# A two-layer graph network: the place of the matrix-sum copy, its add, and the segment sums in the slot order of the edge stage

## The chip, the cores and the metric

The kernel runs on 1 core of one Trainium2 chip. The metric is the device time of one execution in microseconds. The kernel before took 1502.47 us (median of 3 runs, 1501.93 to 1503.01).

## What is computed

The reference has two layers over 1250 nodes with 512 features and 40000 edges, sorted by target node. Only the first is per edge and heavy:

```
h = relu(layernorm(x))
# layer 0
edge_feat = concat(h[src], h[dst], edge_attr)          # 40000 x 1088
m   = mish(mish(edge_feat @ W1 + b1) @ W2 + b2)        # 40000 x 512
agg = segment_sum(m, dst, 1250)
u   = mish(concat(h, agg) @ W3 + b3);  y = h + u @ W4 + b4
x   = x + layernorm(y) * gamma + beta
# layer 1
h   = relu(layernorm(x));  support = (h @ U * s) @ Vt
x   = x + relu(segment_sum(support[src] * w, dst, 1250) + bias)
```

All is float32 on input and output. The kernel multiplies in a rounded 32-bit format and keeps a high and a low part of each operand, so that one product takes three matmuls.

## The kernel before, in words

A prologue works out the node tables `A_tab` (h times the source part of W1) and `Bh_tab`, `Bl_tab` (the target part, high and low). Then comes the **edge stage** (`edge_narrow`, from line 839), which this change touches, then a node stage (W3, W4, norms), and the second layer's matrix product.

The edge stage takes the edges in **groups** of 512, each of 4 **units** of 128: 78 full groups and a tail of 64 edges. A unit number modulo 4 is called j here. Each engine runs its own list of **slots** (`slots`, `step` of each engine), one per unit, and in slot s it works on units at fixed distances from s:

- TensorE, slot s (`step`, L1203): `gathered(s+5)` transposes the gathered table rows into a `bp` bank (4 transposes, L1153), `products(s+5)` adds the two edge products there (L1161, L1165), `msg(s)` makes the second product of the message in bank `bm[j]` (12 matmuls, L1176), `adjacency(s)` adds the unit to the matrix sums in bank `pm` (L1186). After the slot in which a group has been complete for three slots, `seg` makes the group's segment sums in bank `bs` (four f32 products, L1199).
- ScalarE, slot s (`step`, L1285): the first activation of the first mish for unit s+5 (L1235, exp out of `bp`), the first of the second mish for unit s-1 (L1255, exp out of `bm`), then alternately L1259, L1238, L1261, L1241, L1263. Once a group: the cast L1277 (`cast`), the copy of half of the segment sums L1283 (`evac`), and the **copy of the matrix sums** L1270 (`adjacency`: from `pm`, the high parts, to `mev`).
- VectorE, slot s (`step`, L1411): `pre(s+4, 0)` ends the first mish (L1362, waits for ScalarE's L1241), `bias` refills a `bm` bank with b2 (L1381), `square` (L1352, between ScalarE's L1235 and L1238), `pre(s+4, 1)` (L1368), the one-hot columns for the matrix (L1387, L1388), `msg(s-2)` (L1375). Once a group: L1335, L1330, L1342, the add of the segment sums L1409 (`evac`), and the **add of the matrix sums** L1398 (`join`: `mev` += the low parts in `pm`, waits for the copy L1270).
- GpSimd, slot s: the low part `hTl` (L1078), the gathers (L1065), and the adds of `ev` and `mev` into the tables `agg_tab` (L1092) and `M_tab` (L1103) in HBM.

There is one bank `pm`: TensorE's first `adjacency` of a group (j = 0) waits until the join of the group before it is done (`wait(e, s_mev, u.group())`, L1184). There is one bank `bs`: `seg` waits for the add of the group before (`s_ev`, L1197). The order inside a slot is written out by hand in the `step` functions; the lags are the constants in lines 853 to 871. In slot terms, the copy L1270 of group g is issued in ScalarE's slot 4g+4, after L1235 of that slot, and the join in VectorE's slot 4g+4, after L1362 and L1381.

After the last unit, TensorE's slots MSGS and MSGS+1 (313 and 314) hold `xpart(e, 0, 0)` and `xpart(e, 0, 1)`, 12 matmuls each of the node stage (L336). The last full group's `seg` has its slot among them.

Of the kernel before, what the change touches and what calls it, by code (L numbers as in the profile page):

```python
# [34 lines left out]
SUB = 4  # L35
G = SUB * P
NG = -(-E // G)
FULL = E // G
# [800 lines left out]
def edge_narrow(work, scope, sem, k):  # L839
# [13 lines left out]
    PRE_AHEAD = 5  # L853
    ACT_MSG = 1
    DVE_PRE = 4
    DVE_MSG = 2
    SEG_LAG = 3
    CAST_AHEAD = 10
    PREP_AHEAD = {1: 10, 2: 9}
    NEAR_CAST = 8  # L860
# [6 lines left out]
    ACCS = 2  # L867
    MBUF = 2 * SUB
    ADJ_AHEAD = 1
    ADJ_EV_LAG = 4  # L870
    ADJ_LAG = {2: (6, 0), 0: (8, 1)}
    BACK = 2
    FIRST, LOOP0 = -10, 16
# [2 lines left out]
    PRES = 4 * NG  # L876
    MSGS = 4 * FULL + 1
# [3 lines left out]
    with st:  # L881
# [48 lines left out]
        def first(u):  # L930

            return u.reg is None and u.const < SUB
# [9 lines left out]
        def pick(u, start, steady):  # L942

            return start[u.const] if first(u) else steady[u.const % 2]
# [11 lines left out]
        def tail(u):  # L956

            return u.reg is None and u.const >= 4 * FULL
# [184 lines left out]
        @work.on("tensor")  # L1143
        def _(e):
            def gathered(u):
                j, p, w, bank = u.j, u.par, ETAIL if tail(u) else G, pick(u, start_bank, bp)
                if not first(u):
                    e.wait_ge(v_pre, free(u))
                if j == 0:
                    e.wait_ge(q_ga[p], u.pair(64, 16 if tail(u) else 64))  # L1150
                for t in range(SUB if w == G else 1):
                    r = min(P, w)
                    e.matmul(bank[:, t * P:t * P + r].bitcast(F32R), xg[p][0:r, t, j * P:(j + 1) * P], ident_r[0:r, 0:r],  # L1153
                             start=t == 0, stop=False, is_transpose=True, skip_group_check=True)

            def products(u):
                j, p, w, bank = u.j, u.par, ETAIL if tail(u) else G, pick(u, start_bank, bp)
                if j == 0:
                    e.wait_ge(q_win[p], u.pair(48, 48))
                    e.wait_ge(s_hot, u.group(1, 1))  # L1160
                e.matmul(bank[:, 0:w], eaW1[p][:, j * P:(j + 1) * P], M1[p][:, 0:w], start=False, stop=False,  # L1161
                         skip_group_check=True)
                if j == 0:
                    e.wait_ge(s_ealow, u.group(1, 1))
                e.matmul(bank[:, 0:w], eaW2[:, j * P:(j + 1) * P], M2[p][:, 0:w], start=False, stop=True,  # L1165
                         skip_group_check=True).then_inc(s_pre, 1)

            def msg(u):
                j, p, r = u.j, u.par, ETAIL if tail(u) else P
                e.wait_ge(v_bias, u.val(1, 1))  # L1170
                bank = bm[j]
                for c in range(KC):
                    if j == 0:
                        e.wait_ge(g_pre, u.val(1, c + 1))
                    for a, w in ((hTh, W2h), (hTl, W2h), (hTh, W2l)):
                        last = e.matmul(bank[0:r, :], a[p][:, c, j * P:j * P + r], w[:, c, :], start=False,  # L1176
                                        stop=c == KC - 1 and w is W2l, skip_group_check=True)
                last.then_inc(s_msg, 1)

            def adjacency(u):  # L1180

                i, r, o = u.const % 2, ETAIL if tail(u) else P, u.j // HSUB * 2 * EC
                if u.j == 0:
                    wait(e, s_mev, u.group())  # L1184
                e.wait_ge(v_adj, u.val(2, 2))
                e.matmul(pm[0:KEYS, o:o + 2 * EC], key[i][0:r, :], so[i][0:r, :, :].rearrange("p a n -> p (a n)"),  # L1186
                         start=u.j % HSUB == 0, stop=u.j % HSUB == HSUB - 1 or tail(u), skip_group_check=True)\
                 .then_inc(s_adj, 1)

            def seg(u):  # L1190

                p, last, r = u.par, tail(u), ETAIL if tail(u) else P
                n = 1 if last else SUB
                first = u + (1 - n)
                e.wait_ge(v_msg, u.val(1, 1))
                e.wait_ge(s_oh, u.group(1, 1))
                wait(e, s_ev, u.group())  # L1197
                for j in range(n):
                    m = e.matmul(bs[j * WIN:(j + 1) * WIN, :], oh[p][0:r, j, :], tm[(first.const + j) % MBUF][0:r, :],  # L1199
                                 start=True, stop=True)  # L1200
                m.then_inc(s_seg, 1)

            def step(s):  # L1203
                if (s + PRE_AHEAD).has(PRES):
                    gathered(s + PRE_AHEAD)
                    products(s + PRE_AHEAD)
                if s.has(MSGS):
                    msg(s)
                    adjacency(s)
                q = s + -SEG_LAG  # L1210
                if (q.j == SUB - 1 and q.has(4 * FULL)) or (q.reg is None and q.const == 4 * FULL):
                    seg(q)
                if s.reg is None and s.const in (MSGS, MSGS + 1):
                    xpart(e, 0, s.const - MSGS)

            e.wait_ge(c_tb, 3 * (NCH - 2) + 1)
            for j in range(SUB):
                gathered(At(None, j))
            for j in range(SUB):
                products(At(None, j))  # L1220
            slots(e, SUB - PRE_AHEAD, LOOP0, LOOP1, LAST, step)
            e.wait_ge(v_msg, MSGS)
            e.wait_ge(s_mev, NG)

        @work.on("scalar")
        def _(e):
# [58 lines left out]
            def step(s):  # L1285
                u, m, q, g = s + PRE_AHEAD, s + -ACT_MSG, s + -EV_LAG, s + -ADJ_EV_LAG
                c = s + CAST_AHEAD
                if near(s, NEAR_CAST):
                    c = s + NEAR_CAST
                for pre, k in ((1, 0), (0, 0), (0, 1), (1, 2), (0, 2), (1, 3), (0, 3)):  # L1290
                    if pre and u.has(PRES):
                        pre_chain(u, k)
                    if pre and k == 0 and g.j == 0 and g.has(MSGS):
                        adjacency(g)
                    if pre and k == 3 and c.j == 0 and c.has(4 * NG) and (c.reg is not None or c.const >= 4 * SUB
                                                                          or near(s, NEAR_CAST)):
                        cast(c)
                    if not pre and m.has(MSGS):
                        msg_chain(m, k)
                    if not pre and k == 0 and q.j == 0 and q.has(4 * FULL):  # L1300
                        evac(q)
# [19 lines left out]
        def _(e):  # L1321
# [72 lines left out]
            def join(u):  # L1394

                e.wait_ge(a_adj, u.group(1, 1))
                to, of = matrix(u, 1)
                e.tensor_tensor(to, of, to, ALU.add).then_inc(s_mev, 1)  # L1398
# [10 lines left out]
                e.tensor_tensor(ev[u.par][:], bs[n:2 * n, :], ev[u.par][:], ALU.add).then_inc(s_ev, 1)  # L1409

            def step(s):  # L1411
                u, m, v, f, a = s + DVE_PRE, s + -DVE_MSG, s + PRE_AHEAD, s + -(DVE_MSG + 1), s + -ADJ_EV_LAG
                if u.has(PRES):
                    pre(u, 0)
                if f.has(MSGS - SUB):
                    bias(f)
                if a.j == 0 and a.has(MSGS):
                    join(a)
                if v.has(PRES):
                    square(v)  # L1420
                if u.has(PRES):
                    pre(u, 1)
                for k in (1, 2):
                    g = s + PREP_AHEAD[k]
                    if near(s, NEAR_PREP[k]):
                        prep(s + NEAR_PREP[k], k)
                    elif g.j == 0 and g.has(4 * NG) and (g.reg is not None or g.const >= 4 * SUB):
                        prep(g, k)
                h = s + -ONE_LAG
                if h.j == 0 and h.has(MSGS) and not (h.reg is None and h.const <= SUB):  # L1430
                    onehot(h)
                if (s + ADJ_AHEAD).has(MSGS) and not (s.reg is None and s.const == 0):
                    adjacency(s + ADJ_AHEAD)
                if m.has(MSGS):
                    msg(m)
                q = s + -(EV_LAG + 2)
                if q.j == 0 and q.has(MSGS):
                    if tail(q):
                        e.wait_ge(s_seg, NG)
                        e.sem_inc(s_fin, 1)  # L1440
                    evac(q)
                if s.reg is None and s.const == MSGS - 3:
                    split_w3x(e)
# [25 lines left out]
            u = [At(None, j) for j in range(SUB + 1)]  # L1469
# [1059 lines left out]
```

## Time and profile before

| | |
|---|---|
| median of 3 runs | 1502.47 us |
| the profiled execution | 1502.91 us |
| its span in the trace | 1501.1 us |
| mean granted TensorE clock | 0.996 |
| PE busy | 1460.7 us (97%) |
| DVE busy | 1389.8 us (93%) |
| ACT busy | 1343.5 us (89%) |
| POOL busy | 1067.0 us (71%) |

PE is TensorE's matmuls, PEld its weight loads, DVE VectorE, ACT ScalarE, POOL GpSimd, SP SyncE. The busy shares overlap: the engines work side by side on different units. The profiled execution took 1.8 us more than its span, which is what lies around the program. The edge stage's loop fills the span from about 100 to 1375 us.

### The profile page before, as it was taken

What the parts mean: (1) busy time and instruction counts of PE and PEld (TensorE: products, weight loads), DVE (VectorE), ACT (ScalarE), POOL (GpSimd) and SP (SyncE); (2) the same over time, 40 slices, a digit from 0 to 9 for tenths busy, and PEclk for the clock granted to TensorE, in tenths of its full rate; (3) what the DMA queues carried; (4) which work ended last, traced back from release to release, by engine and by line L of the source; (5) the groups of instructions that cost most, each with busy time, mean ns of one, the idle gap of its engine ahead of it and who ended that gap; (6) DMA issues with size and microseconds to landing.
All of it is one profiled execution on the core that took longest, in us unless ns stands there. A gap on an engine that the chain in (4) does not pass through costs nothing.

```text
span 1501.1 us, 33053 instructions
## 1 busy us (share of the span) xinstructions
PE 1460.7 (97%) x7549; PEld 1124.8 (75%) x7549; DVE 1389.8 (93%) x2922; ACT 1343.5 (89%) x2587; POOL 1067.0 (71%) x978
## 2 busy tenths in 40 slices
PE   7989999999999999999999999999999999999998
PEld 6867777777777777777777777777777777777885
DVE  7879999999999999999999999999999999997776
ACT  5098999999999999999999999999999999997562
POOL 1267888788888878887887888778788888863220
PEclk9999999999999999999999999999999999999999
DMA  8867555454555545455545545554554555454764
GB/s 290 273 205 191 121 120 117 116 124 114 122 119 123 116 114 126 114 120 117 128 114 116 124 117 118 118 128 114 118 123 118 117 117 125 117 130 107 180 154 155
DMA packets 126036, 201.90 MB, mean 134 GB/s; under 512 B 32897, under 2 KB 58649, under 8 KB 126000
## 3 DMA queue, kind: packets, MB, share of 16 engines
q0 software_dynamic: 58528, 109.71, 33.8%
q1 hardware_dynamic: 67120, 91.24, 20.2%
q10 hardware_dynamic: 352, 0.52, 0.1%
q8 instruction: 16, 0.26, 0.1%
q14 instruction: 20, 0.16, 0.0%
HBM read 151.60 MB, written 39.54 MB: 127 GB/s over the span
## 4 chain that ended last, share of the span: by engine, by line
PE 76%; issue 8%; POOL 7%; ACT 3%; DVE 2%; POOLq 2%; DMA 1%; SPq 1%; DVEq 0%; ACTq 0%
PE bm L1176 43%; PE bp L1153 5%; PE bp L1161 5%; PE bs L1199 4%; PE bp L1165 4%; PE pm L1186 3%; PE pA L723 2%; PE po L2185 2%; PE pu L336 2%; PE pu L2163 2%; PE pB L723 2%; POOL hTl L1078 2%; POOL agg_tab L1092 2%; POOL xg L1065 2%; POOL M_tab L1103 2%
## 5 line engine op out<-in xcount | busy, mean ns | idle before, releaser
L1078 POOL TENSOR_TENSOR hTl<-tp,hTh 128x512 fp32r<-128x512 f32 (+1 forms) x314 | 410.7, 1308 | 196.5 <-DVE so L1388 193.8
L1176 PE MATMUL bm<-W2h,hTh 128*128 128x512 f32 x1252 | 494.4, 395 | 0.1
L1176 PE MATMUL bm<-W2h,hTl 128*128 128x512 f32 x1252 | 489.9, 391 | 0.0
L1176 PE MATMUL bm<-W2l,hTh 128*128 128x512 f32 x1252 | 489.5, 391 | 0.0
L1065 POOL DMA_INDIRECT xg<-A_tab,idx x305 | 320.7, 1051 | 71.0 <-issue 43.6
L1176 PEld LDWEIGHTS bm<-W2h,hTh 128*128 128x128 f32 x1252 | 235.4, 188 | 62.4 <-POOL hTl L1078 9.3
L1176 PEld LDWEIGHTS bm<-W2l,hTh 128*128 128x128 f32 x1252 | 235.6, 188 | 52.2
L1176 PEld LDWEIGHTS bm<-W2h,hTl 128*128 128x128 f32 x1252 | 235.8, 188 | 47.9
L1362 DVE SCALAR_TENSOR_TENSOR tp<-rp,bp 128x512 f32<-128x512 f32 (+1 forms) x314 | 213.0, 678 | 37.3 <-ACT rp L1241 28.8
L1352 DVE SCALAR_TENSOR_TENSOR rp<-rp 128x512 f32<-128x512 f32 (+1 forms) x314 | 214.9, 685 | 9.2 <-ACT rp L1235 2.7
L1238 ACT ACTIVATE rp<-rp 128x512 f32<-128x512 f32 (+1 forms) x314 | 195.3, 622 | 27.3 <-DVE rp L1352 23.3
L1375 DVE SCALAR_TENSOR_TENSOR tm<-rm,bm 128x512 f32<-128x512 f32 x313 | 211.6, 676 | 2.5 <-ACT rm L1263 2.5
L1381 DVE COPY bm<-b2b 128x512 f32<-128x512 f32 x309 | 211.6, 685 | 0.0
L1235 ACT ACTIVATE rp<-bp 128x512 f32<-128x512 f32 (+1 forms) x314 | 180.2, 574 | 30.5 <-PE bp L1165 30.5
L1259 ACT ACTIVATE rm<-rm 128x512 f32<-128x512 f32 x313 | 197.6, 631 | 7.5
L1263 ACT ACTIVATE rm<-rm 128x512 f32<-128x512 f32 x313 | 193.8, 619 | 0.1
L1261 ACT ACTIVATE rm<-rm 128x512 f32<-128x512 f32 x313 | 193.5, 618 | 0.1
L1241 ACT ACTIVATE rp<-rp 128x512 f32<-128x512 f32 (+1 forms) x314 | 192.8, 614 | 0.1
L1153 PEld LDWEIGHTS bp<-ident_r,xg 128*128 128x128 f32 (+1 forms) x1244 | 130.0, 140 | 78.9 <-issue 36.0
L1255 ACT ACTIVATE rm<-bm 128x512 f32<-128x512 f32 x313 | 183.6, 587 | 0.1
L1092 POOL DMA_DIRECT2D agg_tab<-ev x157 | 157.6, 1004 | 17.2 <-DMA agg_tab<-ev 9.7
L1103 POOL DMA_DIRECT2D M_tab<-mev x157 | 150.8, 961 | 12.6 <-issue 11.6
(248 smaller groups left out, 2196.4 us busy)
## 6 DMA issues: line engine op xcount, KB each, us to landing
ea<-in_eaT SPq DMA_DIRECT2D x156, 128.0 KB
agg_tab<-ev POOLq DMA_DIRECT2D x157, 64.0 KB, 5.1
db<-in_dst_rows SPq DMA_DIRECT2D x78, 128.0 KB
M<-M SPq DMA_DIRECT2D x76, 128.0 KB
M_tab<-mev POOLq DMA_DIRECT2D x157, 60.0 KB, 6.4
M_tab<-zero SPq DMA_DIRECT2D x10, 640.0 KB
xg<-A_tab,idx POOLq DMA_INDIRECT x313
eaW<-Bh_tab SPq DMA_DIRECT2D x77, 64.0 KB
```

The costliest lines, as they stand in the source:

```text
L1065: e.indirect_dma_start(out=xg[p][0:r, t, :].bitcast(F32), out_offset=None, in_=A_d, in_offset=bass.IndirectOffsetOnAxis(ap=idx[p][0:r, t:t ...
L1078: e.tensor_tensor(hTl[p][:, j, 0:w], pick(u, start_t, tp)[:, 0:w], hTh[p][:, j, 0:w], ALU.subtract)\
L1153: e.matmul(bank[:, t * P:t * P + r].bitcast(F32R), xg[p][0:r, t, j * P:(j + 1) * P], ident_r[0:r, 0:r], start=t == 0, stop=False, is_trans ...
L1176: last = e.matmul(bank[0:r, :], a[p][:, c, j * P:j * P + r], w[:, c, :], start=False, stop=c == KC - 1 and w is W2l, skip_group_check=True)
L1238: e.activation(t, t, ACT.Ln, bias=1.0, scale=0.5 / (SQ * SQ)).then_inc(a_pre, 1)
L1259: e.activation(t, t, ACT.Square, bias=SQ, scale=SQ).then_inc(a_msg, 1)
L1261: e.activation(t, t, ACT.Ln, bias=0.5, scale=0.5 / (SQ * SQ)).then_inc(a_msg, 1)
L1263: e.activation(t, t, ACT.Exp, scale=-1.0).then_inc(a_msg, 1)
L1352: e.scalar_tensor_tensor(t, t, 2.0 * SQ, t, ALU.add, ALU.mult).then_inc(v_sq, 1)
L1362: e.scalar_tensor_tensor(t, pick(u, start_r, rp)[:, 0:w], 1.0, pick(u, start_bank, bp)[:, 0:w], ALU.subtract, ALU.mult).then_inc(v_pre, 2 ...
L1375: e.scalar_tensor_tensor(tm[m.const % MBUF][0:r, :], rm[m.const % 2][0:r, :], 1.0, bm[m.j][0:r, :], ALU.subtract, ALU.mult).then_inc(v_msg, 1)
L1381: e.tensor_copy(bm[m.j][:, :], b2b[:]).then_inc(v_bias, 1)
```

## The change

- TensorE: the segment sums of a group stand in the slot after the one they stood in, behind the transposes (`gathered`) and before the edge products (`products`). Before, they stood at the end of the slot before, ahead of these same transposes.
- ScalarE: the matrix-sum copy stands at the end of slot 4g+3, behind L1263, where it stood in slot 4g+4 behind L1235.
- VectorE: the join stays in slot 4g+4 and stands between L1362 and L1381, where it stood behind L1381.

```
-    SEG_LAG = 3
+    SEG_LAG = 4
...
-    ADJ_EV_LAG = 4
+    ADJ_EV_LAG = 3
+    JOIN_LAG = 4
...
             def step(s):                                   # TensorE
                 if (s + PRE_AHEAD).has(PRES):
                     gathered(s + PRE_AHEAD)
+                q = s + -SEG_LAG
+                if (q.j == SUB - 1 and q.has(4 * FULL)) or (q.reg is None and q.const == 4 * FULL):
+                    seg(q)
+                if (s + PRE_AHEAD).has(PRES):
                     products(s + PRE_AHEAD)
                 if s.has(MSGS):
                     msg(s)
                     adjacency(s)
-                q = s + -SEG_LAG
-                if (q.j == SUB - 1 and q.has(4 * FULL)) or (q.reg is None and q.const == 4 * FULL):
-                    seg(q)
                 if s.reg is None and s.const in (MSGS, MSGS + 1):
                     xpart(e, 0, s.const - MSGS)
...
                     if pre and u.has(PRES):                # ScalarE
                         pre_chain(u, k)
-                    if pre and k == 0 and g.j == 0 and g.has(MSGS):
+                    if not pre and k == 3 and g.j == 0 and g.has(MSGS):
                         adjacency(g)
...
-                u, m, v, f, a = s + DVE_PRE, s + -DVE_MSG, s + PRE_AHEAD, s + -(DVE_MSG + 1), s + -ADJ_EV_LAG
+                u, m, v, f, a = s + DVE_PRE, s + -DVE_MSG, s + PRE_AHEAD, s + -(DVE_MSG + 1), s + -JOIN_LAG
                 if u.has(PRES):                            # VectorE
                     pre(u, 0)
+                if a.j == 0 and a.has(MSGS):
+                    join(a)
                 if f.has(MSGS - SUB):
                     bias(f)
-                if a.j == 0 and a.has(MSGS):
-                    join(a)
                 if v.has(PRES):
                     square(v)
```

## Rows read from the trace of the kernel before

**Rows 1.** The page, the chain that ended last, by engine.
```profile
PE 76%; issue 8%; POOL 7%; ACT 3%; DVE 2%; POOLq 2%; DMA 1%; SPq 1%; DVEq 0%; ACTq 0%
```

**Rows 2.** Engines by stretch: busy us of each, granted clock, DMA share, GB/s.
```profile
172.00:1291.00 1119.00, 1102.69 (x5715) 845.35 (x5713) 1082.20 (x2246) 1093.03 (x2111) 903.73 (x817) 1.00 0.51 119
...
1400.00:1501.10 101.10, 94.63 (x559) 74.92 (x557) 71.24 (x181) 42.46 (x87) 16.42 (x16) 0.99 0.58 153
```

**Rows 3.** Waits from 400 to 1200 us: engine, line, releaser: us, times, longest.
```profile
PEld pm L1186 <- issue: 32.8, 49, 0.7
...
DVE tp L1362 <- ACT rp L1241: 16.0, 49, 0.3
ACT rp L1238 <- DVE rp L1352: 13.8, 48, 0.3
PEld bs L1199 <- issue: 12.2, 48, 0.3
PEld bm L1176 <- POOL hTl L1078: 6.0, 27, 0.3
```

**Rows 4.** VectorE's add of the matrix sums by source line: count, duration, first to last.
```profile
L1398 DVE TENSOR_TENSOR mev<-pm,mev x79: 292/414/427, 101.2 to 1374.7; 120x256 f32<-120x256 f32 x78, 120x128 f32<-120x128 f32 x1
```

**Rows 5.** Timeline, VectorE, one group: start, us, what, [idle before <-releaser].
```profile
706.84 0.68 DVE L1352 SCALAR_TENSOR_TENSOR rp<-rp 128x512 f32<-128x512 f32 x1
...
710.78 0.69 DVE L1352 SCALAR_TENSOR_TENSOR rp<-rp 128x512 f32<-128x512 f32 x1
...
713.93 0.69 DVE L1362 SCALAR_TENSOR_TENSOR tp<-rp,bp 128x512 f32<-128x512 f32 x1 [0.34 <-ACT rp L1241]
714.54 0.69 DVE L1381 COPY bm<-b2b 128x512 f32<-128x512 f32 x1
715.13 0.41 DVE L1398 TENSOR_TENSOR mev<-pm,mev 120x256 f32<-120x256 f32 x1
715.46 0.68 DVE L1352 SCALAR_TENSOR_TENSOR rp<-rp 128x512 f32<-128x512 f32 x1
...
717.98 0.69 DVE L1362 SCALAR_TENSOR_TENSOR tp<-rp,bp 128x512 f32<-128x512 f32 x1
```

**Rows 6.** Timeline, ScalarE, the same group.
```profile
707.55 0.63 ACT L1238 ACTIVATE rp<-rp 128x512 f32<-128x512 f32 x1 [0.24 <-DVE rp L1352]
...
710.17 0.58 ACT L1235 ACTIVATE rp<-bp 128x512 f32<-128x512 f32 x1
...
713.17 0.63 ACT L1241 ACTIVATE rp<-rp 128x512 f32<-128x512 f32 x1
713.69 0.63 ACT L1263 ACTIVATE rm<-rm 128x512 f32<-128x512 f32 x1
714.21 0.58 ACT L1235 ACTIVATE rp<-bp 128x512 f32<-128x512 f32 x1
714.69 0.37 ACT L1270 ACTIVATE mev<-pm 120x256 f32<-120x256 f32 x1
...
716.18 0.63 ACT L1238 ACTIVATE rp<-rp 128x512 f32<-128x512 f32 x1
```

**Rows 7.** Timeline, TensorE, the last matmul of msg(j = 0) and what follows.
```profile
715.06 0.39 PE L1176 MATMUL bm<-W2l,hTh 128*128 128x512 f32 x1
715.68 0.38 PE L1186 MATMUL pm<-so,key 128*120 128x256 f32 x1 [0.23 <-issue]
```

**Rows 8.** Timeline, the end of the edge stage.
```profile
1372.77 1.06 PE L1199 MATMUL bs<-tm,oh 128*32 128x512 f32 x8
...
1373.90 0.59 ACT L1283 ACTIVATE ev<-bs 64x512 f32<-64x512 f32 x1 [1.67 <-PE bs L1199]
...
1375.11 0.69 DVE L1409 TENSOR_TENSOR ev<-bs,ev 64x512 f32<-64x512 f32 x1
...
1376.76 1.04 PE L1199 MATMUL bs<-tm,oh 64*32 64x512 f32 x2
```

**Rows 9.** The chain in order of time, one block of 12 matmuls in the node stage.
```profile
1378.83 2.79 PE pu L336 x12
```

More of the change, by code:

```diff
@@ L856, in edge_narrow @@
     DVE_MSG = 2
-    SEG_LAG = 3
+    SEG_LAG = 4
     CAST_AHEAD = 10
@@ L869, in edge_narrow @@
     ADJ_AHEAD = 1
-    ADJ_EV_LAG = 4
+    ADJ_EV_LAG = 3
+    JOIN_LAG = 4
     ADJ_LAG = {2: (6, 0), 0: (8, 1)}
@@ L1205, in step @@
                     gathered(s + PRE_AHEAD)
+                q = s + -SEG_LAG
+                if (q.j == SUB - 1 and q.has(4 * FULL)) or (q.reg is None and q.const == 4 * FULL):
+                    seg(q)
+                if (s + PRE_AHEAD).has(PRES):
                     products(s + PRE_AHEAD)
@@ L1209, in step @@
                     adjacency(s)
-                q = s + -SEG_LAG
-                if (q.j == SUB - 1 and q.has(4 * FULL)) or (q.reg is None and q.const == 4 * FULL):
-                    seg(q)
                 if s.reg is None and s.const in (MSGS, MSGS + 1):
@@ L1292, in step @@
                         pre_chain(u, k)
-                    if pre and k == 0 and g.j == 0 and g.has(MSGS):
+                    if not pre and k == 3 and g.j == 0 and g.has(MSGS):
                         adjacency(g)
@@ L1411, in step @@
             def step(s):
-                u, m, v, f, a = s + DVE_PRE, s + -DVE_MSG, s + PRE_AHEAD, s + -(DVE_MSG + 1), s + -ADJ_EV_LAG
+                u, m, v, f, a = s + DVE_PRE, s + -DVE_MSG, s + PRE_AHEAD, s + -(DVE_MSG + 1), s + -JOIN_LAG
                 if u.has(PRES):
                     pre(u, 0)
+                if a.j == 0 and a.has(MSGS):
+                    join(a)
                 if f.has(MSGS - SUB):
                     bias(f)
-                if a.j == 0 and a.has(MSGS):
-                    join(a)
                 if v.has(PRES):
```

## The prediction

> **What bounds the kernel now.** I first read which engine the page's chain runs over: TensorE for 76% of the span [rows 1]. Then the stretches: from 172 to 1291 us TensorE is busy 1102.69 of 1119 us, ScalarE 1093.03 and VectorE 1082.20 [rows 2]. Three engines within 2% of each other cannot be told apart by shares, so the waits decide. In 800 us of the loop, 49 groups, TensorE has one large repeated wait: the weight load of the matrix sum `pm`, once a group, 32.8 us in all [rows 3]. But VectorE waits too, 49 times and for ScalarE alone (L1362 for L1241, 16.0 us), and ScalarE waits 48 times and for VectorE alone (L1238 for L1352, 13.8 us) [rows 3]. No wait of either for TensorE stands in that view. Two engines that wait for each other once a group, and for nobody else, are a loop that sets the pace; TensorE, which waits for them, has room.
>
> One group, followed by its starts, shows the loop [rows 5, 6]. VectorE's square for j = 2 runs from 706.84 to 707.52. ScalarE starts L1238 at 707.55 and then has no idle time until L1241 of j = 3 ends at 713.17 + 0.63 = 713.80. VectorE, idle for 0.34 us, starts L1362 at 713.93, then L1381 at 714.54, the join at 715.13, the square L1352 at 715.46, which ends at 716.14. ScalarE's L1238 starts at 716.18, 0.04 later, and leads to VectorE's L1362 at 717.98. From there VectorE runs back to back to the next square of j = 2. **The four VectorE instructions L1362, L1381, L1398, L1352 of slot 4g+4 all lie on this loop.** The join runs once a group, 79 times from 101.2 to 1374.7 us, so a group takes 1273.5 / 78 = 16.33 us [rows 4].
>
> TensorE's wait in the same group: the last matmul of msg(j = 0) starts at 715.06. Twelve such matmuls take 2.79 us elsewhere, 0.23 each [rows 9], so `pm` could start at 715.29. It starts at 715.68 [rows 7], 0.14 us after the join's end at 715.13 + 0.41 = 715.54 [rows 5]. The loss is 0.39 us a group.
>
> **The change part by part.**
>
> *Copy, earlier on ScalarE.* It now follows L1263 directly. L1263 starts at 713.69 and the next instruction 0.52 later, at 714.21 [rows 6], so the copy starts at 714.21 and, at 0.37 us [rows 6], ends at 714.58. Before, it ended at 715.06. ScalarE has the same instructions in the same stretch: what the copy pushes, L1235 by some 0.26 us, feeds the square L1352 that starts only at 715.46 and had finished at 714.79, so it ends near 715.05 and is still in time. Its input, the matrix sums of j = 3, is made before TensorE begins the twelve matmuls that end at 715.29, so before 712.5. Cost on ScalarE: nothing, covered by the wait for the square.
>
> *Join, ahead of L1381 on VectorE.* The four instructions keep their sum (713.93 to 715.46, 1.53 us) if the join can start when L1362 lets it, at 714.54 [rows 5]. It can't quite: the copy ends at 714.58, and then comes the way from engine to engine. Two rows bound that. L1235 ends at 710.17 + 0.58 = 710.75 and the square behind it starts at 710.78, 0.03 later; L1241 ends at 713.80 and L1362 starts at 713.93, 0.13 later [rows 5, 6]. So the join starts at 714.61 to 714.71, and the square behind it is late by **0.07 to 0.17 us**. Before, the same wait cost nothing, because L1381 stood between and lasted until 715.13, when the copy had just ended at 715.06. I take the middle, 0.12, since neither row is nearer: at 713.93 VectorE had been idle, at 710.78 it hadn't, and here its L1362 is just ending. The loop has nothing to absorb it, for ScalarE's L1238 already starts 0.04 after the square ends. Some 75 of the 78 groups run in this state: 75 x 0.12 = **9.0 us** lost; ends 5.3 and 12.8.
> Who waits behind the join: L1381 refills a bank with b2 for TensorE's next msg. It now ends at 714.66 + 0.33 + 0.69 = 715.68; TensorE, after `pm` at 715.29, has two 512-column products of 0.23 and four transposes to do first, so it comes after 715.75. Nothing, by a small margin, and on an engine with room.
>
> *What TensorE gains.* The join now ends at about 714.66 + 0.41 = 715.07, before 715.29: the 0.39 us wait at `pm` goes. But TensorE is ahead of the loop by that much afterwards and cannot finish early: VectorE and ScalarE wait for nothing it makes. Late next is the low part `hTl`, for which TensorE's msg of j = 0 already waits in 27 of 49 groups, 6.0 us [rows 3]; it should take over most of the 0.4 us. Gain: 0.
>
> *Segment sums behind the transposes.* Past four transposes, some 0.3 us later. The load of the one-hot weights then waits 0.25 us before it (12.2 us in 48 times) [rows 3], as it would at either place. Between nothing and 0.4 us a group on TensorE, either way, by the size of its other gaps; I take nothing, as the 0.39 us that `pm` sets free covers it. Without that cover it would cost up to 0.4 us a group. The transposes come earlier, and wait for L1362 of the slot before, which has ended by then. Of those who take the sums, ScalarE's L1283 never waited for TensorE in the loop [rows 3]; 0.3 us later should leave it so. No DMA is moved and no queue is passed.
>
> *The end of the loop.* Here the new lag matters once. The last full group's sums stood between the two x parts of the node stage, at 1372.77; now they stand behind both, and the tail's sums directly behind them. They start at 1372.77 + 2.79 = 1375.56 [rows 8, 9]. From their start to the end of L1409 took 1375.80 - 1372.77 = 3.03 us [rows 8], and the tail's sums must wait for that: 1378.59, and 0.13 for the way, 1378.72, against 1376.76 before. That is **2.0 us** in which TensorE has no other work. TensorE is busy 94.63 of the last 101.1 us [rows 2], so the node stage gives little back. Bounds 1.5 to 2.2.
>
> **Sum:** 9.0 + 2.0 = 11.0 us (ends 6.8 and 15.0), on the profiled execution's own 1502.91: 1513.9. The median of the runs shown is 0.4 lower, so I name 1513.5, which is 0.7% slower.
>
> A rule speaks against this. The row shows TensorE with the highest busy time, 98.5% of the stretch, and a bubble of 0.39 us in each group [rows 2, 7]. The Trainium skill ("Perfetto Trace Analysis", section "Identifying Performance Opportunities") says to improve the engine with the highest occupancy, finding its repeated gaps and making what they wait for come sooner, which is what is done here; it warns that matmul occupancy is a poor measure. By that rule the bubble would be time won, which is the first rival.
>
> **The rivals.**
> 1. *TensorE sets the pace* and the bubble was real: 78 x 0.39 = 30.4 us less, the 2.0 at the end more: 1474.5, or 1474 against the median. For it: the chain on TensorE for 76% [rows 1]. Against: that chain stays on a busy engine, and neither VectorE nor ScalarE waits for TensorE anywhere in 49 groups [rows 3]. It decides if waits of theirs that the view can't show, shorter than the overlap of two instructions, hang on TensorE: from 11.0 / 75 = 0.15 us a group given back, the kernel is no longer slower. Smaller gains of that kind fall here too. Chance 0.13.
> 2. *No change*: the join meets the copy in time, or the 0.1 us is absorbed, as it would be if ScalarE, not the square, released L1238. Only the end is left, 2.0 us: 1504.5. For it: the copy ends only 0.04 us after the join could start. Chance 0.15.
> 3. *The segment sums cost TensorE more than it has to spare* and it becomes the bound: a cost of 0.7 us a group against 0.39 set free would be 78 x 0.3 = 24 us, 1528. No row speaks for it beyond the 0.25 us weight load. Chance 0.04.
>
> **How the numbers follow.** The forecast (a wait for the copy on the loop, and the late end) has 0.68. About 0.2%, 3 us, is what a measurement of this kernel can tell from no change. Faster 0.13 from the first rival; same 0.15 from the second; slower 0.72 from the forecast and the third. The range takes the forecast's own ends, 1509 to 1518, and reaches down through the second rival to 1503; outside lie the first, the third and a little.
>
> **What would show it.** Right: the join waits 0.1 us for the copy, with a short gap or a start 0.68 to 0.78 after L1362's; ScalarE's wait at L1238 behind the join grows by as much; a group takes 16.45 us instead of 16.33; TensorE's wait at `pm` is gone and one at `hTl` has grown; the tail's segment sums start 3 us after the last full group's, with TensorE idle between. Wrong: VectorE's wait at L1362 for L1241 shrinks and the group gets shorter; then TensorE was in the loop. If the join starts 0.60 after L1362, the second rival holds.

## The result, and the profile after

The changed kernel takes 1506.24 us (median of 12 runs, 1504.11 to 1508.43), the kernel before 1502.62 us (12 runs, 1501.78 to 1503.02): a ratio of 1.0025, 95% interval 1.0017 to 1.0033. It is 3.6 us slower where 11.0 was forecast. The sign and the range hold, the size doesn't. The profiled execution of the changed kernel took 1506.37 us with a span of 1504.7, against 1502.91 and 1501.1.

Lines of the kernel shift in the changed one: L1362 is L1364, L1352 is L1354, L1381 is L1383, L1398 is L1400 (the join), L1270 is L1272 (the copy), L1263 is L1265, L1241 is L1243, L1238 is L1240, L1199 is L1200 (segment sums), L1186 is L1187.

First the stretches of [rows 2], in the same columns (us, then PE, PEld, DVE, ACT and POOL busy, granted clock, DMA share, GB/s):

```profile
172.00:1291.00 1119.00, 1112.46 (x5718) 851.56 (x5717) 1082.36 (x2246) 1092.83 (x2110) 903.42 (x817) 1.00 0.52 119
...
1400.00:1504.70 104.70, 98.19 (x578) 77.78 (x577) 73.84 (x185) 45.86 (x92) 19.99 (x18) 0.99 0.58 149
```

VectorE and ScalarE are busy as long as before within 0.3 us. TensorE is shown busy 10 us more, for about as many matmuls (5718 and 5715): its ends are modelled, so this is not more work. The waits from 400 to 1200 us, to hold against [rows 3]:

```profile
PEld bp L1162 <- issue: 40.3, 48, 0.8
...
PEld bm L1177 <- POOL hTl L1079: 23.9, 49, 0.7
DVE tp L1364 <- ACT rp L1243: 15.9, 49, 0.3
ACT rp L1240 <- DVE rp L1354: 13.9, 48, 0.3
```

The two waits of VectorE and ScalarE for each other are the same to 0.1 us. The wait at `pm` is gone, and the one for `hTl` has grown from 6.0 to 23.9 us, in each group now, by 0.37 us a group. The first line is the load of the edge products behind the segment sums; before, the transposes stood there and waited as long.

The join and the copy in one group (timeline: start, duration, what):

```profile
713.77 0.63 ACT L1243 ACTIVATE rp<-rp 128x512 f32<-128x512 f32 x1
714.29 0.37 ACT L1272 ACTIVATE mev<-pm 120x256 f32<-120x256 f32 x1
714.54 0.69 DVE L1364 SCALAR_TENSOR_TENSOR tp<-rp,bp 128x512 f32<-128x512 f32 x1 [0.34 <-ACT rp L1243]
714.56 0.63 ACT L1265 ACTIVATE rm<-rm 128x512 f32<-128x512 f32 x1
...
715.14 0.42 DVE L1400 TENSOR_TENSOR mev<-pm,mev 120x256 f32<-120x256 f32 x1
...
715.48 0.68 DVE L1383 COPY bm<-b2b 128x512 f32<-128x512 f32 x1
...
716.07 0.68 DVE L1354 SCALAR_TENSOR_TENSOR rp<-rp 128x512 f32<-128x512 f32 x1
```

The copy stands *ahead* of L1265, not behind it. It ends at 714.66, half a microsecond before the join, which starts 0.60 after L1364, at its earliest. From L1364 to L1354 it is 1.53 us, exactly as before [rows 5]. So the loop is unchanged, and the loss must lie elsewhere. The joins that start between 400 and 700 us, before and after (count, duration, first to last start), say the same:

```profile
L1398 DVE TENSOR_TENSOR mev<-pm,mev x19: 411/414/417, 402.6 to 698.7; 120x256 f32<-120x256 f32 x19
L1400 DVE TENSOR_TENSOR mev<-pm,mev x19: 417/418/420, 402.7 to 698.7; 120x256 f32<-120x256 f32 x19
```

Eighteen groups take 296.1 and 296.0 us, 16.45 us each in both kernels. (The prediction's 16.33 is an average over all 78, in which the last few groups are much shorter; 16.45 is the steady group, and some of the expectations below use it.) The first x part of the node stage, behind the last unit, starts at 1369.79 in both traces, so all that is lost comes after it. The end of the stage, to hold against [rows 8]:

```profile
1375.57 1.07 PE L1200 MATMUL bs<-tm,oh 128*32 128x512 f32 x8
1376.71 0.59 ACT L1285 ACTIVATE ev<-bs 64x512 f32<-64x512 f32 x1 [4.03 <-PE bs L1200]
...
1377.91 0.69 DVE L1411 TENSOR_TENSOR ev<-bs,ev 64x512 f32<-64x512 f32 x1
1378.75 1.57 PE L1200 MATMUL bs<-tm,oh 64*32 64x512 f32 x2 [2.11 <-DVE ev L1411]
```

The sums of the last full group start at 1375.57 (1375.56 was worked out), the tail's at 1378.75 (1378.72), which is 1.99 us later than before. And the tail's sums take 1.57 us where they took 1.04. The next view says why (stretches, columns as above, granted clock third from the end):

```profile
1372.00:1379.10 7.10, 4.99 (x25) 2.92 (x24) 1.76 (x4) 1.40 (x4) 3.25 (x4) 1.00 0.35 37
1379.20:1382.40 3.20, 3.20 (x11) 2.10 (x10) 0.92 (x2) 0.74 (x2) 0.79 (x1) 0.50 0.37 69
1382.60:1400.00 17.40, 17.40 (x81) 14.23 (x80) 10.62 (x17) 12.43 (x19) 4.01 (x5) 1.00 0.97 292
```

After its wait of 2.1 us TensorE was granted half its clock (0.50, the 1.2 GHz level) for some 3.4 us in this execution, with work in front of it: up to 3.4 / 2 = 1.7 us lost. 2.0 + 1.7 is the 3.6 us, within 0.1.

### The profile page after: what moved, and what is told of

It is laid out like the page before. It is cut to its first block, busy times and chain, and to the rows that moved or that the text cites. A ratio compares the mean times of both kernels' runs of the same rounds, so it can differ in the third digit from the quotient of the medians.

```text
span 1504.7 us, 33053 instructions
## 1 busy us (share of the span) xinstructions
PE 1472.2 (98%) x7549; PEld 1132.6 (75%) x7549; DVE 1389.0 (92%) x2922; ACT 1343.1 (89%) x2587; POOL 1066.0 (71%) x978
## 3 DMA queue, kind: packets, MB, share of 16 engines
HBM read 151.60 MB, written 39.54 MB: 127 GB/s over the span
## 4 chain that ended last, share of the span: by engine, by line
POOL 36%; issue 32%; PE 18%; POOLq 9%; ACT 2%; DMA 1%; DVE 1%; SPq 1%; DVEq 0%; ACTq 0%
POOL agg_tab L1093 9%; POOL xg L1066 9%; POOL hTl L1079 9%; POOL M_tab L1104 9%; POOLq L1098 4%; PE bm L1177 4%; POOLq L1084 3%; PE pA L723 2%; PE po L2187 2%; PE pu L336 2%; PE pB L723 2%; PE pu L2165 2%; PE pu L2232 1%; POOLq L1104 1%; PE bs L1200 1%
## 5 line engine op out<-in xcount | busy, mean ns | idle before, releaser
L1364 DVE SCALAR_TENSOR_TENSOR tp<-rp,bp 128x512 f32<-128x512 f32 (+1 forms) x314 | 213.0, 678 | 36.9 <-ACT rp L1243 29.0
L1354 DVE SCALAR_TENSOR_TENSOR rp<-rp 128x512 f32<-128x512 f32 (+1 forms) x314 | 212.9, 678 | 10.4 <-ACT rp L1237 4.0
L1240 ACT ACTIVATE rp<-rp 128x512 f32<-128x512 f32 (+1 forms) x314 | 195.1, 621 | 24.9 <-DVE rp L1354 24.8
L1383 DVE COPY bm<-b2b 128x512 f32<-128x512 f32 x309 | 211.5, 684 | 0.0
L1265 ACT ACTIVATE rm<-rm 128x512 f32<-128x512 f32 x313 | 193.8, 619 | 0.1
L1263 ACT ACTIVATE rm<-rm 128x512 f32<-128x512 f32 x313 | 193.6, 618 | 0.1
L1243 ACT ACTIVATE rp<-rp 128x512 f32<-128x512 f32 (+1 forms) x314 | 192.7, 614 | 0.1
L1154 PEld LDWEIGHTS bp<-ident_r,xg 128*128 128x128 f32 (+1 forms) x1244 | 132.0, 141 | 38.2 <-issue 24.9
```

The lines of the kernel that those rows point to most:

```text
L1240: e.activation(t, t, ACT.Ln, bias=1.0, scale=0.5 / (SQ * SQ)).then_inc(a_pre, 1)
L1265: e.activation(t, t, ACT.Exp, scale=-1.0).then_inc(a_msg, 1)
L1354: e.scalar_tensor_tensor(t, t, 2.0 * SQ, t, ALU.add, ALU.mult).then_inc(v_sq, 1)
L1364: e.scalar_tensor_tensor(t, pick(u, start_r, rp)[:, 0:w], 1.0, pick(u, start_bank, bp)[:, 0:w], ALU.subtract, ALU.mult).then_inc(v_pre, 2 ...
L1383: e.tensor_copy(bm[m.j][:, :], b2b[:]).then_inc(v_bias, 1)
```

## The experiments

The theory to test: the loop of VectorE and ScalarE sets the pace, TensorE has room, and all the loss is at the end of the edge stage. The rival above all: TensorE sets the pace, and the new place of the segment sums eats what `pm` gives. Each ratio is to the kernel before, run beside it.

### The parts alone

The copy and the join alone (segment sums with `SEG_LAG = 3`, at the end of the slot as before):

```
     SEG_LAG = 3
-    ADJ_EV_LAG = 4
+    ADJ_EV_LAG = 3
+    JOIN_LAG = 4
```

> The kernel before with the copy and the join moved as in the change, the segment sums left where they were. Theory (the loop between VectorE and ScalarE sets the pace and the join starts 0.60 us behind L1364, as in the changed kernel; all the loss is at the end of the edge stage): a group takes the same 16.45 us although TensorE no longer waits at pm, the end is that of before, so the time is that of before, 1502.6 us within 1. Rival (TensorE sets the pace, and in the changed kernel the segment sums' new place eats what pm gives): 1472 to 1490 us.

1502.27 us against 1502.33, ratio 1.0000 (0.9991 to 1.0009). The waits from 400 to 1200 us:

```profile
PEld bm L1177 <- POOL hTl L1079: 33.3, 49, 0.8
...
DVE tp L1363 <- ACT rp L1242: 16.0, 49, 0.3
ACT rp L1239 <- DVE rp L1353: 13.9, 48, 0.3
```

The gap at `pm` is closed and nothing is gained: nearly all of the wait has moved to `hTl` (33.3 us, where `pm` had 32.8 and `hTl` 6.0). The rival's 12 us or more are excluded. (A group takes 16.45 us here as before.)

The segment sums alone (the copy and the join as before):

```
-    SEG_LAG = 3
+    SEG_LAG = 4
```

with `seg` moved between `gathered` and `products`.

> The kernel before with the segment sums alone moved (new lag, between transposes and products). Theory: the loop is untouched, the end has the 2.0 us wait of TensorE between the last two segment sums, and in some executions a lower clock behind it: 1504.5 to 1507 us, as the changed kernel. Rival (the sums' place costs TensorE something in every group, which only the free pm hides): pm is waited for here as before, so the groups get longer, by 0.1 us or more each, 8 us in all: 1512 us or more.

1505.85 us, ratio 1.0021 (1.0012 to 1.0031). This part makes the whole difference (3.5 of the 3.6 us), and the 1512 of the rival isn't there: with `pm` waited for as before, the groups don't get longer. In this profiled execution (1504.95 us) the tail's sums start after the same wait, and the clock stays up behind it:

```profile
1378.79 1.02 PE L1199 MATMUL bs<-tm,oh 64*32 64x512 f32 x2 [2.11 <-DVE ev L1410]
```

### The end mended

```
-                if (q.j == SUB - 1 and q.has(4 * FULL)) or (...):
+                if (q.j == SUB - 1 and q.has(4 * FULL - 1)) or (...):
                     seg(q)
...
+                if s.reg is None and s.const == MSGS + 1:
+                    seg(At(None, 4 * FULL - 1))
                 if s.reg is None and s.const in (MSGS, MSGS + 1):
                     xpart(e, 0, s.const - MSGS)
```

> The changed kernel, with the last full group's segment sums put back between the two x parts, where they stood before. Theory: TensorE does not idle at the end, its clock stays up, and all of the 3.6 us comes back: 1502.6 us within 1. Rival (the loss lies in the loop or in the start of the stage): at most 1 us comes back, 1505 us or more.

1503.15 us, ratio 1.0007 (0.9998 to 1.0016). Of the 3.6 us, 2.8 come back (against the 1502.33 beside it). The last 0.8 us is within the interval of nothing; whether the sums' place in the loop costs 0.01 us a group can't be told from this.

### The gap filled with idle work

Nine products that nobody reads, in TensorE's 2 us wait:

```
                     seg(q)
+                    if q.reg is None and q.const == 4 * FULL - 1:
+                        for _ in range(9):
+                            e.matmul(bm[3][:, :], W2h[:, 0, 0:P], W2h[:, 1, :], start=True, stop=True)
```

> The changed kernel with nine matmuls of 512 columns, whose result nobody uses, between the last full group's segment sums and the tail's, in the 2 us in which TensorE waits. Theory (the wait costs 2.0 us by itself, and the clock falls to half after it in some executions, which costs up to 1.7 us more): the 2.0 us stay, the half-clock stretch behind the wait is gone: 1504.5 us, with a spread as small as that of before. Rival (the clock's fall has nothing to do with the idle time): the clock falls as often as in the changed kernel and the time is 1506.2 us.

1504.16 us, ratio 1.0011 (1.0002 to 1.0019): 2.1 us less than the changed kernel, with more work, or 1.7 us by the kernel before beside each (1.9 us over it here, 3.6 there); the two intervals overlap slightly. The wait itself stays: the tail's sums start 3.26 us after the last full group's (1373.90 to 1377.16). The profile has no half-clock stretch at this place:

```profile
1379.20:1382.40 3.20, 3.20 (x19) 2.63 (x18) 1.88 (x3) 2.58 (x3) 0.77 (x1) 1.00 0.61 200
```

The spread was to be as small as that of before (1.2 us) and is 2.7, so that part of the expectation missed. The kernel before, run beside it, spread over 5.4 us (1501.10 to 1506.48 in 35 runs), so the spread tells little. One thing besides the gap varies in the traces: the mean clock from 125 to 145 us, at the start of the stage, is 0.91 before, 0.83 in the changed kernel and 1.00 in this one, whose x part starts 1.7 us earlier for it or for something else (1368.12 against 1369.79).

The traces can be freed of that by counting from the start of the first x part to the end of the span:

| kernel | gap | half clock behind it | x part from | span | between, us |
|---|---|---|---|---|---|
| before | no | no | 1369.79 | 1501.1 | 131.3 |
| copy and join alone | no | no | 1369.55 | 1500.9 | 131.4 |
| end mended | no | no | 1370.23 | 1501.6 | 131.4 |
| gap filled | filled | no | 1368.12 | 1501.5 | 133.4 |
| segment sums alone | yes | no | 1369.83 | 1503.2 | 133.4 |
| changed | yes | 3.4 us | 1369.79 | 1504.7 | 134.9 |
| copy behind L1265 (below) | yes | 6.8 us | 1378.26 | 1514.7 | 136.4 |

The wait costs 2.1 us whether TensorE idles in it or not, the half clock behind it 1.5 us for 3.4 us of it and 3.1 for 6.8. The 6.8 us come from that trace's mean clock, 0.69 from 1384 to 1392 us and 0.77 from 1392 to 1396: 5.0 and 1.8 us at the half.

### The prediction's term, put where it was said to be

The copy behind the last message activation of the slot:

```
-                    if not pre and k == 3 and g.j == 0 and g.has(MSGS):
-                        adjacency(g)
...
                     if not pre and m.has(MSGS):
                         msg_chain(m, k)
+                    if not pre and k == 3 and g.j == 0 and g.has(MSGS):
+                        adjacency(g)
```

> The changed kernel with the matrix-sum copy where the prediction had put it by mistake, behind the last message activation of the slot instead of ahead of it. Prediction's term: the join then waits for the copy, 0.07 to 0.17 us in each of 75 groups on the loop of VectorE and ScalarE: 5 to 13 us more than the changed kernel, 1511 to 1519 us, and a group of 16.52 to 16.62 us. Rival (the loop has slack that absorbs 0.1 us): 1506 us as the changed kernel.

1513.8 us, ratio 1.0075 (1.0061 to 1.0089): 7.6 us more than the changed kernel. One group:

```profile
718.71 0.62 ACT L1265 ACTIVATE rm<-rm 128x512 f32<-128x512 f32 x1
718.95 0.69 DVE L1364 SCALAR_TENSOR_TENSOR tp<-rp,bp 128x512 f32<-128x512 f32 x1 [0.34 <-ACT rp L1243]
719.23 0.37 ACT L1272 ACTIVATE mev<-pm 120x256 f32<-120x256 f32 x1
...
719.63 0.43 DVE L1400 TENSOR_TENSOR mev<-pm,mev 120x256 f32<-120x256 f32 x1
...
720.57 0.68 DVE L1354 SCALAR_TENSOR_TENSOR rp<-rp 128x512 f32<-128x512 f32 x1
```

The copy ends at 719.60, the join starts 0.03 later and 0.68 after L1364, and L1364 to L1354 takes 1.62 us instead of 1.53. No idle time is shown: a wait of 0.08 us hides in the overlap of two instructions. 7.6 us over 78 groups is 0.10 each, within the 0.07 to 0.17 of the prediction; the joins from 405.3 to 686.6 us, 17 groups, are 16.55 us apart instead of 16.45. The kernel that the prediction described is this one. That its time is also the forecast's, 1513.5, is in part luck: the loop lost 7.6 us where 9.0 were said, and the end 3.6 or more where 2.0 were.

### How much room TensorE has

The 256-column product of `pm` repeated three times in one slot of each group (eight in the second kernel), with the same result:

```
+                for _ in range(3 if u.j == 2 else 0):
+                    e.matmul(pm[0:KEYS, o:o + 2 * EC], key[i][0:r, :], so[i][0:r, :, :]...,
+                             start=True, stop=False, skip_group_check=True)
```

> The kernel before with the 256-column product of pm repeated three times in slot j = 2 of each group (same operands, same result): 3 x 0.12 us = 0.35 us more of TensorE work a group. Theory (TensorE has about 0.4 us to spare, which it spends waiting at pm): absorbed, 1502 us within 2, and the wait at pm shrinks. Rival (TensorE sets the pace): 78 x 0.35 = 27 us more, 1529 us.

> The same with eight repeats, 0.93 us more a group, over what TensorE has to spare. Theory: 0.4 to 0.6 us of it absorbed, the rest shows: 78 x (0.3 to 0.5) = 26 to 40 us more, 1528 to 1542 us, and the wait at pm is gone. Rival (TensorE sets the pace): 72 us more, 1575 us.

Three: 1502.97 us, ratio 1.0007 (0.9997 to 1.0016). Eight: 1535.78 us, ratio 1.0226 (1.0209 to 1.0243), 33.7 us more. Waits from 400 to 1200 us, three repeats and then eight:

```profile
PEld pm L1189 <- issue: 16.3, 49, 0.4
DVE tp L1365 <- ACT rp L1244: 16.1, 49, 0.3
ACT rp L1241 <- DVE rp L1355: 13.9, 49, 0.3
```

```profile
DVE rp L1355 <- ACT rp L1238: 23.2, 48, 0.5
ACT rp L1241 <- DVE rp L1355: 14.2, 48, 0.3
ACT rp L1238 <- PE bp L1165: 13.9, 48, 0.3
```

0.35 us more work a group vanishes, and the wait at `pm` halves by it (32.8 to 16.3 us in 49 groups is 0.34 each). Of 0.93 us, 0.43 show (33.7 / 78) and 0.5 are absorbed, and only here, of all the kernels of this document, does ScalarE wait for TensorE between 400 and 1200 us (third line), once a group. That is what a trace looks like in which TensorE is on the path.

### Shortening the loop itself

ScalarE waits 0.24 us a group at L1238 of slot j = 2 while its cast stands behind, on the loop. The kernel before with the cast moved ahead of that wait:

```
-                    if pre and k == 3 and c.j == 0 and c.has(4 * NG) and (...):
-                        cast(c)
...
                         evac(q)
+                    if not pre and k == 0 and c.j == 0 and c.has(4 * NG) and (...):
+                        cast(c)
```

> The kernel before with ScalarE's cast of the edge features (once a group, in slot j = 2) moved ahead, from behind L1241 to behind the first message activation, where ScalarE has 0.14 us between two activations of one tile and then waits 0.24 us for VectorE's square. Theory (VectorE and ScalarE wait for each other and set the pace): 0.2 to 0.5 us a group off the loop, 15 to 38 us: 1465 to 1487 us, and TensorE's wait at pm shrinks. Rival (TensorE sets the pace): no change, 1502.6 us.

> As the last, with the change's copy and join but the segment sums where they were. If with the early cast the wait at pm still holds the join's place in the loop, this gains over the last by up to the 0.39 us a group (30 us) that TensorE lost there; if VectorE's own work is what is left as the bound, it is the same as the last within 2 us.

> The changed kernel, the end mended, with the early cast. Against the last this has only the segment sums between transposes and products. If TensorE is now near its own limit, the difference is what the sums' place costs or gives on TensorE, in my estimate within 0.1 us a group, 8 us either way; if VectorE is the bound, the same as the last within 1 us.

1500.69 us (ratio 0.9989, 0.9980 to 0.9998), 1501.55 (1.0005, 0.9991 to 1.0019) and 1502.43 (1.0000, 0.9991 to 1.0009). The first is the fastest complete kernel here, by 0.1%, and the expected 15 us or more aren't there. The other two don't improve on it (the second ran from 1500.19 to 1509.30, three of its twelve runs above 1508). By the time alone this is what the rival foretold. The groups of instructions from 400 to 1200 us (count | busy us, mean ns | idle before), before and with the early cast:

```profile
L1078 POOL TENSOR_TENSOR hTl<-tp,hTh 128x512 fp32r<-128x512 f32 x195 | 256.4, 1315 | 117.8 <-DVE so L1388 116.6
L1065 POOL DMA_INDIRECT xg<-A_tab,idx x195 | 203.7, 1044 | 32.1 <-issue 27.2 <-DVE ev L1409 1.5
...
L1352 DVE SCALAR_TENSOR_TENSOR rp<-rp 128x512 f32<-128x512 f32 x194 | 132.7, 684 | 4.1
```

```profile
L1065 POOL DMA_INDIRECT xg<-A_tab,idx x194 | 308.2, 1588 | 32.0 <-issue 31.1
L1078 POOL TENSOR_TENSOR hTl<-tp,hTh 128x512 fp32r<-128x512 f32 x194 | 307.3, 1584 | 19.7 <-DVE so L1388 19.7
L1352 DVE SCALAR_TENSOR_TENSOR rp<-rp 128x512 f32<-128x512 f32 x193 | 155.2, 804 | 0.0
```

VectorE no longer waits at L1362, but GpSimd's gather takes 1588 ns instead of 1044 and its `hTl` 1584 instead of 1315, VectorE's L1352 804 instead of 684, and GpSimd waits for VectorE 19.7 us instead of 116.6. ScalarE still waits at L1238, and for longer (24.9 us instead of 13.8). The growth of L1352 is one long instance a group, and it is the one behind the join, on the loop:

```profile
708.33 0.41 DVE L1398 TENSOR_TENSOR mev<-pm,mev 120x256 f32<-120x256 f32 x1
708.66 1.14 DVE L1352 SCALAR_TENSOR_TENSOR rp<-rp 128x512 f32<-128x512 f32 x1
709.83 0.63 ACT L1238 ACTIVATE rp<-rp 128x512 f32<-128x512 f32 x1 [0.54 <-issue]
707.57 1.67 POOL L1078 TENSOR_TENSOR hTl<-tp,hTh 128x512 fp32r<-128x512 f32 x1
```

That square starts while GpSimd's subtraction runs, until 709.24, and ends 0.56 us after it (the profile's spans of GpSimd are rough). What the early cast takes off the loop, this square puts back on.

It is not so from the start. The same trace has its joins 15.94 us apart up to 340 us and 16.54 from there on (first two lines). In the first stretch neither instruction is long (the other lines, 170 to 315 us; a gather takes 1043 ns), and GpSimd waits for VectorE a good tenth of the time:

```profile
L1398 DVE TENSOR_TENSOR mev<-pm,mev x9: 402/414/417, 185.1 to 312.6; 120x256 f32<-120x256 f32 x9
L1398 DVE TENSOR_TENSOR mev<-pm,mev x18: 401/403/407, 410.6 to 691.8; 120x256 f32<-120x256 f32 x18
L1078 POOL TENSOR_TENSOR hTl<-tp,hTh 128x512 fp32r<-128x512 f32 x37 | 48.5, 1310 | 17.9 <-DVE so L1388 17.6
L1352 DVE SCALAR_TENSOR_TENSOR rp<-rp 128x512 f32<-128x512 f32 x37 | 25.1, 678 | 0.0
```

So a complete kernel with the early cast does run 0.5 us a group faster than before, for some 14 groups, with TensorE's work unchanged (it is busy 145.0 of the 145 us). Then a gather of GpSimd comes 0.96 us late (at 341.12) and takes 1.90 us, and the pattern with the long square stays for the rest of the loop, 0.09 us a group slower than before. 14 x 0.5 less and some 60 x 0.09 more leave about the 1.6 us that were measured. The other two kernels with the early cast turn at the same group. An add of GpSimd that came as late (at 289.94) had not turned it. Why the pattern holds was not tested. The question put to the next two kernels was simpler: had GpSimd become the bound, or was TensorE? To tell them apart, GpSimd was relieved of its adds into `M_tab`, without and with the early cast. These two leave the matrix of the 78 full groups out, so the second layer's sum is of the tail alone:

```
-                e.dma_start(M_d[...], mev[...], accum_op=ALU.add).then_inc(landed, 16)
+                if landed is q_adj:
+                    e.sem_inc(q_adj, 16)
+                else:
+                    e.dma_start(M_d[...], mev[...], accum_op=ALU.add).then_inc(landed, 16)
```

> The kernel before, with GpSimd's adds of the matrix sums into M_tab (two issues a group, about 1.0 us each on GpSimd) left out for the 78 full groups, so that the second layer's sum is of the tail alone. It frees 2 us of GpSimd a group and nothing else. Theory (in the kernel before VectorE and ScalarE set the pace, GpSimd has room): 1502 us as before, within 2. Rival (GpSimd is part of the bound already): 10 us or more faster.

> As the last, with the cast moved early as in the run e6, whose gain was 1.6 us where 15 to 38 were expected, while GpSimd had no idle time left and its instructions and VectorE's L1352 took longer. The same work is left out. Theory (the early cast does free the loop of VectorE and ScalarE, and GpSimd then takes over as the bound): with GpSimd relieved the gain appears, 0.2 to 0.5 us a group, 15 to 38 us against the last run. Rival (TensorE sets the pace, and that is why the early cast gave nothing): no more than 3 us against the last run.

1500.99 us (ratio 0.9992, 0.9982 to 1.0001) and 1463.67 us (0.9743, 0.9726 to 0.9759). Two microseconds a group taken from GpSimd bring 1 us in all, but with the early cast on top 37.3 us, the upper end of what was expected. The engines from 400 to 1200 us in the last kernel:

```profile
400.00:1200.00 800.00, 798.84 (x4210) 627.68 (x4211) 793.73 (x1656) 796.01 (x1556) 571.35 (x501) 1.00 0.44 115
```

TensorE does as many groups' work in less time, at 99.9% busy. It wasn't the bound at 98.5%. With the adds gone L1352 takes 684 ns again and a group some 16.0 us to the end of the loop, so it is something about these adds that the long square needs. Their time on GpSimd and their traffic (39.54 MB written before, 29.95 here) went together, so which of them is open.

## Why the prediction was right and wrong

**Right: what bounds the kernel.** The loop of VectorE and ScalarE, read from two small waits, sets the pace; closing TensorE's 0.39 us gap a group brought nothing (copy and join alone: ratio 1.0000), extra work of 0.35 us cost nothing, and a TensorE bound only appears with 0.93. The first rival, TensorE as the bound, falls, and so does the outcome of the Trainium skill's rule ("Perfetto Trace Analysis", "Identifying Performance Opportunities") of closing the gaps of the engine with the highest occupancy, when TensorE is picked for it by its matmuls; its own warning, that matmul occupancy is a poor measure, agrees with these traces: 97% before and 98% after, and slower. By the weight loads' busy share, one of the two measures that the section would have instead (75% before and after), TensorE isn't even the busiest here, VectorE (93%) is. What was put on the loop itself showed in every group: 0.08 us of waiting for the copy made it 0.10 us longer, a cast of some 0.5 us taken off made it 0.5 us shorter, as long as that pattern lasted.

**Right: what TensorE's wait turns into.** The wait for `hTl` was named as late next and took over, 6.0 to 23.9 us.

**Wrong: the step "It now follows L1263 directly".** This is the step that failed, and the sentence on the copy in the section on the change ("at the end of slot 4g+3, behind L1263") has the same mistake. In ScalarE's loop over (pre, k) the new test `not pre and k == 3` stands above the call of `msg_chain(m, k)` in the same pass. So the copy is issued ahead of L1263, 0.52 us earlier than was worked out: in the trace it ends at 714.66, 0.12 us after L1364's start and 0.48 before the join's earliest. The join's wait for it, 9.0 of the 11.0 us, doesn't exist. The second rival ("the join meets the copy in time") is what happened in the loop. The size of the term was sound for the order it assumed: 0.10 us a group, 7.6 us in all, measured.

**Right: the end of the loop,** 2.0 us worked out, 1.99 in the trace, and 1.9 in the runs with the gap filled.

**Missing: the clock behind the gap.** A TensorE that idles for 2.1 us was costed at 2.1 us. In the changed kernel's profile half the clock for 3.4 us follows, some 1.5 us more. The runs bear it out as a share: filling the gap takes 1.7 to 2.1 us off the median. That idle time is its cause is shown only so far: of seven profiled executions of kernels with the loop as here, the four without the gap have no such stretch at this place, of the three with it two have it (the changed kernel, 3.4 us, and the copy behind L1265, 6.8 us) and one has not (the segment sums alone). A gap that costs 2.1, 3.6 or 5.1 us would also fit the wide spread of the changed kernel (1504.11 to 1508.43), but only one of its executions was read.

**A reading that could not decide.** "A group takes 16.45 us instead of 16.33" was named as a sign of being right. 16.45 is what a steady group took before, so that length came out with the loop unchanged; a loss of 0.12 us would have made it 16.57.

So 11.0 = 9.0 + 2.0 should have read 3.6 = 0 + 2.0 + 1.6. The range held the result only because it reached down to the second rival.

## What to carry to other kernels

Read which engines wait for each other in every round; take the length of a round from the steady part of the loop, not from its average; if two do and neither waits for the third, the third's gaps are not worth closing, however high its busy share. When the order inside a slot comes from a loop with conditions, write out the emitted sequence for one slot before costing a move, since one place earlier or later decided 9 of 11 us here. And a new lag has to be followed to the last pass of the loop, where the work that covered it ends: the whole loss of this change is there.

## What the runs showed of the hardware

- An engine's wait shorter than the overlap of two instructions shows as no idle time: with the copy behind L1265, VectorE lost 0.08 us at each join, and the waits view from 400 to 1200 us names none. The start-to-start distance (0.68 instead of 0.60) shows it.
- The place of one ScalarE instruction changed durations on engines that weren't touched: with the early cast, from 340 us on, GpSimd's gather went from 1044 to 1588 ns, its subtraction from 1315 to 1584, VectorE's f32 square from 684 to 804 on average (once a group 1.14 us, begun while GpSimd's subtraction ran). In the same execution before 340 us they took 1043, 1310 and 678 ns. So one execution has two patterns that each repeat, 15.94 and 16.54 us a group, and a gather that comes 0.96 us late stands where the one turns into the other. With GpSimd's adds left out as well, the first pattern stays and the kernel is 37 us faster. That VectorE and GpSimd get in each other's way at the memory is argued from this, not shown by itself.
- A TensorE gap of 2.1 us at full clock was followed, in two of three profiles, by a stretch at the 1.2 GHz level with work waiting, 3.4 us in one and 6.8 us in the other; it cost 1.5 and 3.1 us.
